# A two-layer transformer on one core: loads of the set-up, the last expert's order, and the engines of the last norm

## The chip, the cores and the metric

The kernel runs on one core of a Trainium2 chip. A core has TensorE (PE in the views; its weight loads are PEld), VectorE (DVE), ScalarE (ACT), GpSimd (POOL) and SyncE (SP, which here only issues DMAs), and 16 DMA engines that move data between the chip's memory (DRAM) and the on-chip buffers. Each engine works through its own queue in order; queues wait for each other on semaphores. The metric is the device time of one execution in microseconds (us); the number given for a kernel is the median of its runs.

## What is computed

Input is x of 4 sequences of 1024 tokens of 256 features. Two blocks follow each other, with a layer norm after each part (cut to its core):

```python
x = norm(x + attention_window_64(x))              # 16 heads of 16, rotary
x = norm(x + sigmoid(xr @ Wr.T) * (square(relu(xk @ Wk.T)) @ Wv.T))   # xr, xk mix x with its predecessor
x = norm(x + linear_attention(x, Wq, Wk, Wv, Wo, random_features))
# last part, a block of its own:
h  = layernorm(x, ln1);  x = x + causal_attention(h @ Wqkv) @ Wproj
h2 = layernorm(x, ln2);  gates = softmax(h2 @ Wgate);  top 2 of 8 experts, capacity 1024 slots each
y_e  = gelu(h2[slots of e] @ W1[e] + b1[e]) @ W2[e] + b2[e]           # e = 0..7, hidden width 1024
x[token] += gate * y_e[slot];   out = norm(x)
```

## The kernel before, in words

The program is four blocks. At the end of a block all engines meet before the next one starts.

1. **Set-up** (`set_up`, L1815 to L1894). SP issues loads of the first sequence's rows (`b_src`), of weights, tables and small vectors, then of the second sequence's rows (`b_y`), then waits and issues ten more weight loads. DVE fills constants, waits, casts four tables to bf16 and finishes three small constants. PE waits, makes the 128x128 product of the random features (`gram`) and turns the rows of the first sequence with 16 transposes (`turn_tiles`, L1467); ACT takes them out of PSUM (L1478). DVE and PE both wait for all loads that stand ahead of `b_y` (L1856, L1873), SP for the same (L1842).
2. **Attention and the first layers** (`attend_and_pass_on`). A planner with a cost for each step writes out the order of every engine. Its first step on PE is the projection of the first sequence (L834); SP's first is the copy of projected queries and keys into the layout for scores (`b_qk<-b_split`, L688). Nothing in this order is changed, apart from what the section on the change tells.
3. **Experts** (`experts`). Per expert e PE makes the hidden layer in 16 groups of 2 matmuls of 512 columns (L1591; `n` is a tile of hidden features, `h` a half of the 1024 slots, `n` outer and `h` inner; the trace has two records for each matmul), into PSUM banks 0 to 3 in turn. ACT applies Gelu to each group (L1624). Then PE turns the next expert's tokens (L1570), waits for all 16 Gelus and makes the 8 tiles of values (128 slots x 256), two to a PSUM bank (L1600). DVE adds the bias and scales by the gate, pair by pair (L1645, L1650). POOL adds each tile to the rows in DRAM with an indirect DMA (L1553), and before each one waits until the one before has landed (`s.summed`, L1551): 64 of them in one chain over the kernel. At the end POOL waits for the last one and the block ends.
4. **Last norm** (`last_norm`). SP reads 4096 rows back in 8 loads of 512 rows (4 tiles of 128 rows; one such load is here called an eighth). For each eighth DVE makes statistics (L1710, L1713), adds epsilon (L1715), ACT makes the inverse root (L1695, L1697), DVE refines it by one Newton step and makes scales and shifts (L1723 to L1727), and the four tiles are scaled, two by DVE (L1730) and two by ACT (L1688). DVE's order is statistics of eighth h, then scale of eighth h-1. SP stores each eighth (L1677) and waits for the stores.

Of the kernel before, what the change touches and what calls it, by code (L numbers as in the profile page):

```python
# [32 lines left out]
P = 128  # L33
# [544 lines left out]
def attend_and_pass_on(nc, u, s, x_dram, later, early_in, slots_gathered, slots_dram, z_dram, x4_dram):  # L578
# [93 lines left out]
    with nc.Block() as block:  # L672
        @block.sync
        def _(sp):
            for x in plan.program["SP"]:
# [50 lines left out]
        def _(pe):  # L726
            for x in plan.program["PE"]:
# [3 lines left out]
                if kind in LAYER_KINDS:  # L731
# [29 lines left out]
                    elif kind == "pj":  # L761
                        done(pe, b, "o_take", x[1] // 2)
                        pe.wait_ge(s.back_read, order[("keep", plan.group_of(b, True, 0), x[1] // 2)] + 1)
                        if b == 0 and x[1] == 0:
                            pe.wait_ge(later, 16 * len(LATER_WEIGHTS))
# [297 lines left out]
        def _(dve):  # L1063
# [11 lines left out]
            for x in plan.program["DVE"]:  # L1075
                kind = x[0]
                if kind in LAYER_KINDS:
# [381 lines left out]
def turn_tiles(pe, src, u, s, chunks=range(NC), half_ready=None):  # L1459


    for h in range(2):
        if half_ready is not None:
            pe.wait_ge(half_ready, h + 1)
        for c in chunks:
# [54 lines left out]
def experts(nc, u, s, slots_gathered, slots_dram, z_dram, w1_dram, b1_dram, w2_dram, b2_dram, x4_dram):  # L1520
# [3 lines left out]
    gathered = (s.x0_gathered, s.x1_gathered)  # L1524
    with nc.Block() as block:
# [13 lines left out]

        @block.gpsimd  # L1540
        def _(pool):
# [3 lines left out]
            gather_tokens(pool, 1, u, s, z_dram)  # L1545
            for e in range(E_):
                for q in range(4):
                    pool.wait_ge(s.y_done, 4 * e + q + 1)
                    for t in range(2):
                        column = CT * e + 2 * q + t  # L1550
                        if column:  # L1551
# [3 lines left out]
                            in_=u.ye[q][:, t, :], in_offset=None, bounds_check=N + P - 1, oob_is_err=True,  # L1555
                            compute_op=ALU.add).then_inc(s.summed, 16)
                    if q == 0 and e + 2 < E_:
                        pool.wait_ge(s.turned, 4 * (e + 1))
                        gather_tokens(pool, e + 2, u, s, z_dram)
            pool.wait_ge(s.summed, 16 * E_ * CT)  # L1560

        @block.tensor
        def _(pe):
# [14 lines left out]
            turn(0)  # L1578
            for e in range(E_):
                pe.wait_ge(weights_in[e % 2], 32 * (e // 2 + 1))  # L1580
                for n in range(NF):
                    for h in range(2):
                        k = 2 * n + h
                        if n == 0:
                            pe.wait_ge(s.taken, 4 * e + 2 * h + 2)
                        if k >= 4:
                            pe.wait_ge(s.h_done, 16 * e + k - 3)
                        elif e:
                            pe.wait_ge(s.y_added, 4 * (e - 1) + k + 1)
                        for c in range(NC):  # L1590
                            ins = pe.matmul(u.psum[:, k % 4, :], u.w1[e % 2][:, c, P * n:P * n + P],  # L1591
                                            u.xgt[:, c, BANK * h:BANK * h + BANK], start=(c == 0), stop=(c == NC - 1))
                        ins.then_inc(s.h_ready, 1)
                if e + 1 < E_:
                    turn(e + 1)
                pe.wait_ge(s.h_done, 16 * (e + 1))
                for q in range(4):
                    for t in range(2):
                        for n in range(NF):
                            ins = pe.matmul(u.psum[:, q, D * t:D * t + D],  # L1600
                                            u.hid[:, n, P * (2 * q + t):P * (2 * q + t + 1)], u.w2[e % 2][:, n, :],
                                            start=(n == 0), stop=(n == NF - 1))
                    ins.then_inc(s.y_ready, 1)

        @block.scalar
        def _(act):
# [10 lines left out]
            for e in range(E_):  # L1617
                if e:
                    act.wait_ge(s.y_ready, 4 * e)
                for n in range(NF):  # L1620
                    for h in range(2):
                        k = 2 * n + h
                        act.wait_ge(s.h_ready, 16 * e + k + 1)
                        act.activation(u.hid[:, n, BANK * h:BANK * h + BANK], u.psum[:, k % 4, :], ACT.Gelu,  # L1624
                                       bias=u.b1[:, NF * e + n:NF * e + n + 1]).then_inc(s.h_done, 1)
                if e + 1 < E_:
                    take(e + 1)

        @block.vector
        def _(dve):  # L1630
# [8 lines left out]
            dve.wait_ge(s.consts_in, 32)  # L1639
            for e in range(E_):  # L1640
                for q in range(4):
                    dve.wait_ge(s.y_ready, 4 * e + q + 1)
                    if e:
                        dve.wait_ge(s.summed, 16 * (CT * (e - 1) + 2 * q + 2))
                    dve.tensor_tensor(u.ye[q][:, :, :], u.psum[:, q, :].rearrange("p (t d) -> p t d", t=2),  # L1645
                                      u.b2b[:, e:e + 1, :].broadcast_to([P, 2, D]), ALU.add).then_inc(s.y_added, 1)
                    dve.wait_ge(s.y_added, 4 * e + q + 1)
                    for t in range(2):
                        column = CT * e + 2 * q + t
# [326 lines left out]
```

## Time and profile before

| | before |
|---|---|
| median of 3 runs | 1938.33 us (1937.84 to 1943.58) |
| profiled execution | 1937.2 us, span from first to last instruction 1935.3 us |
| busy share of the span | PE 89%, DVE 53%, ACT 46%, POOL 43% |
| mean granted TensorE clock | 0.949 of full speed |

How to read it: 1.9 us of the profiled execution lie outside the span. All positions in time below are in us from the span's start. PE is busy 89% of the whole, but there are stretches at either end in which it does nothing. Of the 40 slices of the profile page (48.4 us each) the first has PE at 4 tenths and the last at 0; all three edits of this change lie in those, and in the slice before the last.

### The profile page before, as it was taken

How to read it: one execution, taken by the hardware profiler on the slowest of the kernel's cores; microseconds unless marked ns; L12 is line 12 of the kernel's file. 1: busy time of each engine (PE TensorE's matmuls, PEld its weight loads, DVE VectorE, ACT ScalarE, POOL GpSimd, SP SyncE). 2: the span in 40 equal slices, each digit the busy share in tenths (PEclk: the TensorE clock that was granted, in tenths of full speed). 3: DMA queues.
4: the chain of work that ended last, by engine and by line, in shares of the span. 5: the costliest groups of instructions: out<-in, count | busy, mean ns of one | idle time of the engine just before them, and what ended most of it. 6: DMA issues, size and time to landing. Idle time of an engine off the chain costs nothing. (4 is left out here: it accounts for less than half of the span.)

```text
span 1935.3 us, 32833 instructions
## 1 busy us (share of the span) xinstructions
PE 1727.9 (89%) x10804; PEld 1102.1 (57%) x10804; DVE 1018.1 (53%) x2375; ACT 886.0 (46%) x1855; POOL 827.1 (43%) x1247
## 2 busy tenths in 40 slices
PE   4798998999999899999999999999269999999980
PEld 3565766565467556547755654555237776666750
DVE  2556677858566885847798677785201110001115
ACT  2354464557755364675546466766032222221212
POOL 4573664422377552237664233423533333334210
PEclk9898999999999899999999999999579999999995
DMA  5615235032444213244502214420323323333115
GB/s 186 88 24 66 34 79 67 13 56 67 58 68 92 29 18 50 67 66 68 104 9 34 34 47 66 68 67 2 110 88 81 83 40 72 76 85 84 22 19 179
DMA packets 93058, 124.17 MB, mean 64 GB/s; under 512 B 14064, under 2 KB 63152, under 8 KB 92736
## 3 DMA queue, kind: packets, MB, share of 16 engines
q1 hardware_dynamic: 78560, 105.24, 26.5%
q0 software_dynamic: 14336, 16.83, 5.3%
q8 instruction: 94, 1.54, 0.4%
q14 instruction: 68, 0.56, 0.1%
HBM read 45.70 MB, written 25.56 MB: 37 GB/s over the span
## 5 line engine op out<-in xcount | busy, mean ns | idle before, releaser
L1013 ACT ACTIVATE b_probs<-b_psum 128x512 f32<-128x512 f32 (+3 forms) x896 | 421.2, 538 | 212.0 <-PE b_psum L881 204.6
L1264 DVE TENSOR_REDUCE b_mneg<-b_psum 128x2 f32<-128x384 f32 (+5 forms) x608 | 335.2, 591 | 124.0 <-PE b_psum L868 121.9
L1359 POOL TENSOR_SCALAR_AFFINE_SELECT b_probs<-b_probs 128x512 f32<-128x512 f32 (+1 forms) x400 | 240.1, 612 | 330.3 <-ACT b_probs L1013 320.2
L868 PE MATMUL b_psum<-b_qk 96*128 96x192 bf16 (+4 forms) x1280 | 300.7, 299 | 2.2 <-DVE b_mhalf L1264 1.1
L881 PE MATMUL b_psum<-b_qk 99*128 99x192 bf16 (+5 forms) x1344 | 270.3, 290 | 13.6 <-DVE b_mneg L1264 4.8
L1645 DVE TENSOR_TENSOR b_ye<-b_psum,b_b2b 128x512 f32<-128x512 f32 x32 | 22.1, 692 | 428.2 <-PE b_psum L1600 428.2
L1624 ACT ACTIVATE b_hid<-b_psum,b_b 128x512 f32<-128x512 f32 x128 | 88.0, 687 | 317.3 <-PE b_psum L1591 317.3
L1553 POOL DMA_INDIRECT before_last_norm<-b_ye,b_ids x64 | 99.6, 1557 | 300.0 <-DMA before_last_norm<-b_ye,b_ids 159.9
L1600 PE MATMUL b_psum<-b_w,b_hid 128*128 128x256 f32 x1024 | 222.4, 379 | 0.8 <-ACT b_hid L1624 0.8
L1591 PE MATMUL b_psum<-b_xgt,b_w 128*128 128x512 f32 x512 | 221.2, 592 | 0.0
L1600 PEld LDWEIGHTS b_psum<-b_w,b_hid 128*128 128x128 f32 x1024 | 193.9, 190 | 27.6 <-ACT b_hid L1624 1.6
L897 PE MATMUL b_psum<-b_probs,b_v 128*32 128x192 f32 (+4 forms) x2688 | 198.9, 417 | 0.3 <-POOL b_probs L1359 0.3
L881 PEld LDWEIGHTS b_psum<-b_qk 99*128 99x128 bf16 x1344 | 113.3, 98 | 118.3 <-issue 30.6
L868 PEld LDWEIGHTS b_psum<-b_qk 96*128 96x128 bf16 x1280 | 125.1, 100 | 90.4 <-issue 23.3
L1264 DVE TENSOR_REDUCE b_mhalf<-b_psum 128x1 f32<-128x512 f32 x256 | 165.1, 681 | 17.6 <-PE b_psum L868 17.0
L1375 POOL TENSOR_TENSOR b_rot<-b_product 128x128 f32<-128x128 f32 x256 | 111.5, 468 | 126.1 <-DVE b_product L1247 62.8
L1591 PEld LDWEIGHTS b_psum<-b_xgt,b_w 128*128 128x128 f32 x512 | 97.4, 191 | 119.0 <-issue 118.6
L1247 DVE TENSOR_TENSOR b_product<-b_psum,b_cossin 128x512 f32<-128x512 f32 x128 | 87.9, 687 | 64.6 <-PE b_psum L834 58.4
L834 PE MATMUL b_psum<-b_wqkv,b_xt 128*128 128x384 f32 x320 | 117.8, 494 | 1.4 <-ACT b_xa L924 0.4
L897 PEld LDWEIGHTS b_psum<-b_probs,b_v 128*32 128x32 f32 x2688 | 69.4, 110 | 85.8 <-issue 67.2
L1381 POOL TENSOR_TENSOR b_split<-b_rest,b_split 128x512 bf16<-128x512 f32 x64 | 74.9, 1173 | 42.2 <-ACT b_split L1032 41.5
L861 PE MATMUL b_psum<-b_mask_q,b_id 128*128 128x384 bf16 (+1 forms) x256 | 85.3, 336 | 7.6 <-DMA b_qk<-b_split 6.2
(212 smaller groups left out, 2444.2 us busy)
## 6 DMA issues: line engine op xcount, KB each, us to landing
b_qk<-b_split SPq DMA_DIRECT2D x372, 128.0 KB, 4.9
b_w<-in_W SPq DMA_DIRECT2D x16, 1024.0 KB, 7.8
b_src<-in_x SPq DMA_DIRECT2D x4, 1024.0 KB, 7.6
before_last_norm<-b_early SPq DMA_DIRECT2D x4, 1024.0 KB, 5.1
b_o<-before_last_norm SPq DMA_DIRECT2D x4, 1024.0 KB, 5.4
before_last_norm<-b_o SPq DMA_DIRECT2D x4, 1024.0 KB, 4.5
normed<-b_y SPq DMA_DIRECT2D x4, 1024.0 KB, 4.5
b_rows<-before_last_norm SPq DMA_DIRECT2D x8, 512.0 KB, 7.7
```

The costliest lines, as they stand in the source:

```text
L834: ins = pe.matmul(u.psum[:, plan.bank[x], 0:384].rearrange("p (a g y) -> p a g y", a=3, g=2), x_rows[:, c, P * t:P * t + P], (u.wqkv0 if n ...
L868: ins = pe.matmul(out[:, i, :], q[0:KS, h, P * t:P * t + P], q[0:KS, HG + h, a:e], start=not last, stop=True, skip_group_check=True)
L881: ins = pe.matmul(out[:, i, :], q[0:KM, HG + h, P * t:P * t + P], q[0:KM, h, a:e], start=True, stop=True, skip_group_check=True)
L897: ins = pe.matmul(u.ot[32 * h:32 * h + 32, a:e], u.v[:, g % 4, t, (HD + 1) * h:(HD + 1) * h + 32], probs_of(cell, a, e)[:, h, :], start=(t ...
L1013: act.activation(probs_of((g, h2, t), a, e)[:, heads[0]:heads[-1] + 1, :], bank, ACT.Exp, scale=SCALE).then_inc(s.exp_done, 1)
L1264: dve.tensor_reduce(out, in_bank(("max",) + x[1:], heads, e - a), AX.X, ALU.max, negate=True).then_inc(s.max_read, 1)
L1359: ins = pool.affine_select(out=block, in_=block, pattern=[[0, HG], [1 if ahead else -1, z - y]], compare_op=ALU.is_ge, fill=none, base=y - ...
L1375: ins = pool.tensor_tensor(out[:, :, :, HALF * y:HALF * y + HALF], straight[:, :, :, HALF * y:HALF * y + HALF], crossed[:, :, :, HALF * (1 ...
L1553: pool.indirect_dma_start(out=x4_dram, out_offset=bass.IndirectOffsetOnAxis(ap=u.ids[:, column:column + 1], axis=0), in_=u.ye[q][:, t, :], ...
L1591: ins = pe.matmul(u.psum[:, k % 4, :], u.w1[e % 2][:, c, P * n:P * n + P], u.xgt[:, c, BANK * h:BANK * h + BANK], start=(c == 0), stop=(c ...
L1600: ins = pe.matmul(u.psum[:, q, D * t:D * t + D], u.hid[:, n, P * (2 * q + t):P * (2 * q + t + 1)], u.w2[e % 2][:, n, :], start=(n == 0), s ...
L1624: act.activation(u.hid[:, n, BANK * h:BANK * h + BANK], u.psum[:, k % 4, :], ACT.Gelu, bias=u.b1[:, NF * e + n:NF * e + n + 1]).then_inc(s ...
```

## The change

**Set-up.** The identity (`b_id`) and the first sequence's rows in two halves are issued first and have semaphores of their own; PE turns the rows as each half lands, before it makes `gram`. What DVE and `gram` wait for is five loads: `wqkv0`, `cossin`, `blocks`, the tables and the random features, the last now one DMA that repeats its source in place of eight. Then come `b_y` and the 16 small loads that nothing in the set-up needs, counted on the semaphore `later`. The ten weight loads move into the next block's SP queue, ahead of its first step. DVE's two additions of 1 (`bk`, `bq_plus`) move to the first `y1` step of the first sequence, behind a wait for everything on `later`; PE's wait ahead of the first `pj` covers the same count.

**Last expert.** For e = 7 the hidden groups run with `h` outer: ten groups (all eight of the first half of slots, two of the second), then the values of tiles 0 to 3, then the six other groups, then tiles 4 to 7. The values go to banks 4 to 7 and 0, tiles 6 and 7 are emptied singly. The other seven experts are as before.

**Last norm.** It stands in the experts' block: SP waits for the last landing itself and reads on. The Newton step, the scales and the shifts move from DVE to POOL, as six small operations (the combined one becomes two). Of the four tiles ACT scales two, POOL one, DVE one. DVE's order is statistics of h, then one tile of h-1. The load of ACT's function table stands behind the last Gelu.

```diff
 def turn_tiles(...):
     for h in range(2):
+        pe.wait_ge(rows_in[h], 16 if h else 32)
...
 # set_up, SP
-            sp.dma_start(u.src[:, :, :], ...).then_inc(loaded, 16)
-            for n in names: ...                      # 14 loads
-            ... tables, bk, bv, bo, 8 x rft, slots, 2 x spare_rows, all on loaded
-            ... u.y on early_in
-            sp.wait_ge(loaded, 16 * (count + 3))
-            for n in LATER_WEIGHTS: ...
+            sp.dma_start(u.id32[:, :], a["id32"]).then_inc(rows_in[0], 16)
+            for h in range(2):
+                sp.dma_start(u.src[:, 4 * h:4 * h + 4, :], x_rows[:, 4 * h:4 * h + 4, :]).then_inc(rows_in[h], 16)
+            for n in first:                          # wqkv0 cossin blocks
+                sp.dma_start(made[n][:], a[n]).then_inc(loaded, 16)
+            sp.dma_start(tables, a["tables"]).then_inc(loaded, 16)
+            sp.dma_start(u.rft[:, :].rearrange("p (j d) -> p j d", d=HD), a["rft"].unsqueeze(1).broadcast_to([64, P // HD, HD])
+                         ).then_inc(loaded, 16)
+            ... u.y on early_in; LATER_SMALL, LATER_ROWS, slots, 2 x spare_rows on later
 # set_up, PE
-            pe.wait_ge(loaded, 16 * (count + 3))
-            gram; turn_tiles(pe, u.src, u, s)
+            turn_tiles(pe, u.src, u, s, rows_in)
+            pe.wait_ge(loaded, 16 * count)
+            gram
 # attend_and_pass_on, SP
+            for n in LATER_WEIGHTS:
+                sp.dma_start(made[n][:], arrays[n]).then_inc(later, 16)
             for x in plan.program["SP"]:
 # attend_and_pass_on, DVE, kind y1
+                        if not b and not x[1]:
+                            dve.wait_ge(later, LATER_COUNT)
+                            dve.tensor_scalar(u.bk[:, :], u.bk[:, :], 1.0, None, ALU.add)
+                            chained(dve.tensor_scalar(u.bq_plus[:, :], u.bq[:, :], 1.0, None, ALU.add))
...
 # experts, PE, last expert
+                parts = list(enumerate(hidden_order(e)))
+                for k, (n, h) in parts[:NF + 2]:
+                    hidden(e, k, n, h)
+                pe.wait_ge(s.h_done, 16 * e + NF)
+                for tiles in pieces_of(e)[:2]:
+                    values(e, tiles)
+                for k, (n, h) in parts[NF + 2:]:
+                    hidden(e, k, n, h)
                 pe.wait_ge(s.h_done, 16 * (e + 1))
+                for tiles in pieces_of(e)[2:]:
+                    values(e, tiles)
...
 # experts, SP: the last norm's reads
+            sp.wait_ge(s.summed, 16 * E_ * CT)
+            for h in range(HALVES):
+                sp.dma_start(u.rows[:, 4 * h:4 * h + 4, :], rows(x4_dram, h)).then_inc(rows_in[h], 16)
 # experts, POOL, behind the last scatter
-            pool.wait_ge(s.summed, 16 * E_ * CT)
+            link = dve_chain(pool, last.chain)
+            for h in range(HALVES):
+                pool.wait_ge(last.root_ready, h + 1)
+                link(pool.tensor_tensor(scales, root, root, ALU.mult))
+                ... three more of the Newton step, each behind link
+                link(pool.tensor_tensor(u.shifts[:, four], u.last_mv[:, four, 0], scales, ALU.mult))
+                pool.tensor_scalar(u.shifts[:, four], u.shifts[:, four], -1.0, None, ALU.mult).then_inc(last.scale_ready, 1)
+                i = 4 * h + 2
+                pool.tensor_scalar(u.rows[:, i, :], u.rows[:, i, :], u.last_mv[:, i, 0:1], u.scales[:, i:i + 1],
+                                   ALU.subtract, ALU.mult).then_inc(last.pool_ready, 1)
```

On SP, at the head of the program, this stood before (L1828 to L1844 is the set-up; a name ahead of `<-` is what is written):

```order
L1830 DMA b_src<-in_x 128x8x256
L1832 DMA b_wqkv<-in_wqkv 128x1536
...
L1837 DMA b_rft<-in_rft 64x16 x8
L1838 DMA slots<-in_empty 16x1024
L1840 DMA normed<-in_spare_rows 16x2048
L1840 DMA before_last_norm<-in_spare_rows 16x2048
L1841 DMA b_y<-in_x 128x8x256
L1844 DMA b_wout<-in_wout 128x512
...
L1844 DMA b_wqkv<-in_wqkv 128x1536
L1827 UNCONDITIONAL_BRANCH
```

and this stands there now:

```order
L1866 DMA b_id<-in_id 128x128
L1868 DMA b_src<-in_x 128x4x256 x2
L1870 DMA b_wqkv<-in_wqkv 128x1536
L1870 DMA b_cossin<-in_cossin 128x1024
L1870 DMA b_blocks<-in_blocks 128x128
L1871 DMA b_o<-in_tables 128x768
L1872 DMA b_rft<-in_rft 64x8x16
L1874 DMA b_y<-in_x 128x8x256
...
L1863 UNCONDITIONAL_BRANCH
L679 UNCONDITIONAL_BRANCH
L682 DMA b_wout<-in_wout 128x512
```

The end of the block (the branch) has moved ahead of the ten weight loads; ahead of it stand 25 DMAs now, 41 before.

On PE, the end of the program before (the last expert: 16 groups of hidden, then all values):

```order
L1591 MATMUL b_psum<-b_xgt,b_w 128x512 x32
L1600 MATMUL b_psum<-b_w,b_hid 128x256 x64
L1525 UNCONDITIONAL_BRANCH
```

and now:

```order
L1651 MATMUL b_psum<-b_xgt,b_w 128x512 x20
L1659 MATMUL b_psum<-b_w,b_hid 128x256 x32
L1651 MATMUL b_psum<-b_xgt,b_w 128x512 x12
L1659 MATMUL b_psum<-b_w,b_hid 128x256 x32
```

The same 96 matmuls, with half of the values moved ahead of 12 of the hidden ones.

On POOL, behind the last scatters, where before only the block's end stood, there is now for each eighth:

```order
L1603 DMA before_last_norm<-b_ye,b_ids 4224x256 x22
L1615 TENSOR_TENSOR b_scales<-b_last_root 128x4
L1616 TENSOR_TENSOR b_scales<-b_scales,b_last_var 128x4
L1617 TENSOR_SCALAR b_scales<-b_scales 128x4
L1618 TENSOR_TENSOR b_scales<-b_scales,b_last_root 128x4
L1619 TENSOR_TENSOR b_shifts<-b_last_mv,b_scales 128x4
L1620 TENSOR_SCALAR b_shifts<-b_shifts 128x4
L1622 TENSOR_SCALAR b_rows<-b_rows,b_last_mv,b_scales 128x256
```

Seven operations of an eighth that stood on DVE (five small ones and two tiles) are now seven on POOL and one on DVE.

## Rows read from the trace of the kernel before

**Rows 1.** Waits, 0 to 30 us: total us, times, longest.

```profile
PE b_psum L1874 <- DMA before_last_norm<-in_spare_rows: 19.7, 1, 19.7
```

**Rows 2.** Timeline, 0 to 40 us: start, duration, engine, what, [idle before].

```profile
0.80 0.44 SPq L1830 DMA_DIRECT2D b_src<-in_x  x1
...
10.56 5.05 SPq L1837 DMA_DIRECT2D b_rft<-in_rft  x8
...
20.59 0.28 DVE L1863 TENSOR_TENSOR b_bg<-b_psum,b_blocks 128x128 f32<-128x128 f32 x1
...
24.02 0.45 SPq L1844 DMA_DIRECT2D b_wqkv<-in_wqkv  x1
...
24.99 7.13 PE L834 MATMUL b_psum<-b_wqkv,b_xa 128*128 128x384 f32 x16 [0.94 <-PEq L1827]
...
32.40 2.75 PE L834 MATMUL b_psum<-b_wqkv,b_xa 128*128 128x384 f32 x8
...
36.24 3.85 SPq L688 DMA_DIRECT2D b_qk<-b_split  x6
```

**Rows 3.** Windows: stretch, us, busy per engine, granted clock, DMA share, GB/s.

```profile
0.00:5.00 5.00, 0.00 (x0) 0.00 (x0) 2.63 (x8) 1.28 (x1) 4.40 (x6) 1.00 0.54 172
5.00:10.00 5.00, 0.00 (x0) 0.00 (x0) 0.00 (x0) 0.00 (x0) 5.00 (x2) 1.00 1.05 337
```

**Rows 4.** Timeline of the last expert, 1820 to 1900 us.

```profile
1822.31 27.63 PE L1591 MATMUL b_psum<-b_xgt,b_w 128*128 128x512 f32 x64
...
1850.72 27.89 PE L1600 MATMUL b_psum<-b_w,b_hid 128*128 128x256 f32 x128 [0.78 <-ACT b_hid L1624]
1857.93 0.69 DVE L1645 TENSOR_TENSOR b_ye<-b_psum,b_b2b 128x512 f32<-128x512 f32 x1 [33.89 <-PE b_psum L1600]
...
1860.04 1.54 POOL L1553 DMA_INDIRECT before_last_norm<-b_ye,b_ids  x1 [22.02 <-DVE b_ye L1650]
...
1871.74 0.69 DVE L1645 TENSOR_TENSOR b_ye<-b_psum,b_b2b 128x512 f32<-128x512 f32 x1 [5.55 <-PE b_psum L1600]
...
1878.23 1.59 POOL L1553 DMA_INDIRECT before_last_norm<-b_ye,b_ids  x1 [3.05 <-DMA before_last_norm<-b_ye,b_ids]
...
1891.60 1.54 POOL L1553 DMA_INDIRECT before_last_norm<-b_ye,b_ids  x1 [2.85 <-DMA before_last_norm<-b_ye,b_ids]
1899.65 7.48 SPq L1673 DMA_DIRECT2D b_rows<-before_last_norm  x8
```

**Rows 5.** Timeline of the last norm, 1900 to 1936 us.

```profile
1903.88 1.40 DVE L1710 BATCH_NORM_STATS2 b_last_bn<-b_rows 128x6 f32<-128x256 f32 x4 [23.89 <-DMA b_rows<-before_last_norm]
...
1905.73 0.17 DVE L1715 TENSOR_SCALAR b_last_var<-b_last_mv 128x4 f32<-128x4 f32 x1
...
1906.17 0.20 ACT L1697 ACTIVATE b_last_root<-b_last_ln 128x4 f32<-128x4 f32 x1
...
1909.25 1.40 DVE L1710 BATCH_NORM_STATS2 b_last_bn<-b_rows 128x6 f32<-128x256 f32 x4
...
1912.68 1.40 DVE L1710 BATCH_NORM_STATS2 b_last_bn<-b_rows 128x6 f32<-128x256 f32 x4
...
1930.85 1.09 ACT L1688 ACTIVATE b_rows<-b_rows,b_shifts,b_scales 128x256 f32<-128x256 f32 x2 [0.42 <-DVE b_shifts L1727]
```

**Rows 6.** Timeline, POOL, 582 to 585 us: its small operations, each behind a semaphore.

```profile
582.57 0.25 POOL L1309 CAST b_mparts<-b_mneg 128x16 bf16<-128x16 f32 x1
...
583.55 0.27 POOL L1312 TENSOR_TENSOR b_mparts<-b_mrest,b_mparts 128x16 bf16<-128x16 f32 x1
```

**Rows 7.** One line, L1348 and L1309: count, duration ns min/median/max.

```profile
L1348 POOL TENSOR_SCALAR b_xa<-b_xa x16: 1476/1487/1509, 233.5 to 1100.8; 128x512 f32<-128x512 f32 x16
...
L1309 POOL CAST b_mparts<-b_mneg x64: 248/254/712, 51.6 to 1313.8; 128x16 bf16<-128x16 f32 x64
```

**Rows 8.** Timeline, POOL and DVE, 573 to 578 us: two operations side by side.

```profile
576.40 1.27 POOL L1330 TENSOR_TENSOR b_o<-b_y,b_o 128x512 f32<-128x512 f32 x1
...
576.52 1.18 DVE L1103 TENSOR_SCALAR b_kvm_mt<-b_kvm_mt 128x4 f32<-128x4 f32 x1
```

More of the change, by code:

```diff
@@ L1545, in _ @@
             gather_tokens(pool, 1, u, s, z_dram)
+            piece = 0
             for e in range(E_):
[L1547 to L1550, printed above, removed]
+                for tiles in pieces_of(e):
+                    piece += 1
+                    pool.wait_ge(s.y_done, piece)
+                    for t in tiles:
+                        column = CT * e + t
                         if column:
@@ L1578, in _, with hidden @@
             turn(0)
+            def hidden(e, k, n, h):
+                if n == 0:
+                    pe.wait_ge(s.taken, 4 * e + 2 * h + 2)
+                if k >= 4:
+                    pe.wait_ge(s.h_done, 16 * e + k - 3)
+                elif e:
+                    pe.wait_ge(s.y_added, 4 * (e - 1) + k + 1)
+                for c in range(NC):
+                    ins = pe.matmul(u.psum[:, k % 4, :], u.w1[e % 2][:, c, P * n:P * n + P],
+                                    u.xgt[:, c, BANK * h:BANK * h + BANK], start=(c == 0), stop=(c == NC - 1))
+                ins.then_inc(s.h_ready, 1)
@@ L1579, in _, with values @@
+            def values(e, tiles):
+                for t in tiles:
+                    for n in range(NF):
+                        ins = pe.matmul(u.psum[:, bank_of(e, t), D * (t % 2):D * (t % 2) + D], u.hid[:, n, P * t:P * (t + 1)],
+                                        u.w2[e % 2][:, n, :], start=(n == 0), stop=(n == NF - 1))
+                ins.then_inc(s.y_ready, 1)
             for e in range(E_):
                 pe.wait_ge(weights_in[e % 2], 32 * (e // 2 + 1))
[L1581 to L1593, printed above, removed]
@@ L1605, in _ @@
+                for tiles in pieces_of(e)[2:]:
+                    values(e, tiles)
         @block.scalar
@@ L1708, in statistics @@
+            link = dve_chain(dve, last.dve_chain)
+            def apply(h):
+                dve.wait_ge(last.scale_ready, h + 1)
+                i = 4 * h + 3
+                dve.tensor_scalar(u.rows[:, i, :], u.rows[:, i, :], u.last_mv[:, i, 0:1], u.scales[:, i:i + 1],
+                                  ALU.subtract, ALU.mult).then_inc(last.dve_ready, 1)
+            for h in range(HALVES):
                 dve.wait_ge(rows_in[h], 16)
@@ L1821, in set_up @@
     gram = ctx.enter_context(nc.semaphore("gram_ready"))
-    names = "wqkv0 cossin id32 blocks iota next_token mur muk bq ln1g ln1b ln2g ln2b wgate".split()
-    count = len(names) + 5 + P // HD
+    rows_in = [ctx.enter_context(nc.semaphore(f"first_rows{h}_in")) for h in range(2)]
+    first = "wqkv0 cossin blocks".split()
+    count = len(first) + 2
     bf16_tables = (u.id16[:, :], u.mask_q[:, :, :], u.causal_q[:, :], u.upto[:, :])
@@ L1926, in two_layers @@
             u = named(made)
[L1927 to L1929 removed]
+            experts(nc, u, moe, last, slots_gathered, slots_dram, z_dram, a["W1"], a["b1"], a["W2"], a["b2"], x4_dram, out)
 def kernel(**inputs):
```

195 lines of the change are left out of this document (85 added, 110 removed).

## The prediction

> **What bounds the kernel now.** I read the waits at the start first: PE, which is 89% busy over the whole, stands for 19.7 us until the last of the set-up's loads has landed [rows 1]. Then the timeline of the first 40 us, for what SP does meanwhile: between 0.80 and 10.56 it issues 19 DMAs, one every 0.514 us, and the eight tiny ones of the random features cost it 5.05 us, 0.63 each [rows 2]. The DMA engines are near full from 5 to 10 us (share 1.05, 337 GB/s; 172 GB/s in the first 5) [rows 3], so the bulk is in by about 10 us and what PE waits for afterwards is SP's own pace. The block ends for another reason: SP's tenth weight load goes out at 24.02 and ends at 24.47, and PE's first projection starts at 24.99 [rows 2]. That is the first thing to move.
>
> At the other end I read the timeline of the last expert [rows 4]. PE finishes at 1878.6, but POOL's scatters are a chain, each waiting for the landing of the one before: eight from 1860.04 to 1891.60, one every 4.51 us. They start late because all 16 hidden groups (27.6 us) stand ahead of the first values. From the last issue (1891.60 + 1.54) the landing takes as long as those before it, 2.9 us, so it is in at 1896.05. SP's first read of the norm goes out only at 1899.65: 3.6 us for the end of the block. From there to the end of the span are 35.65 us, and the norm's timeline shows DVE with an eighth every 3.43 us (statistics start 1909.25, 1912.68) [rows 5], without a gap. So the tail is scatter chain, block end, DVE.
>
> **Set-up: −10.2 us.** Ahead of the block's end stand 25 DMAs: 20 of the kind that took 0.514 us, and five (random features, b_y, three with 16 partitions) that I price at 0.63 like the features [rows 2]: 10.3 + 3.2 + 0.8 = 14.3. From SP's last issue to PE's start were 0.5 us (24.47 to 24.99); so PE starts at 14.8, against 24.99. Is anything later than SP? The five loads with rows and identity ahead of them are 2.9 MB; rows 3 give 2.5 MB in the first 10 us, so they are in near 11.5 with the landing, and DVE's casts and `b_bg` behind them took from the release at 19.7 to 20.87, 1.2 us: 12.7. PE's 16 transposes lie ahead of that. SP keeps the block. The ten weight loads, 4.9 us of SP, now run from about 14.8 to 19.7; the first thing behind them, the copies to b_qk at 36.24, comes at 26 at the earliest, so they cost nothing there, and their 3.1 MB take 9.2 us at 337 GB/s, over by 25. DVE's two moved additions (under 0.5 us together) and its new wait come over 100 us later, when all this has long landed. Bounds: without any queueing it is 10.6. If DMAs of many pieces hold SP up as the eight reads of the norm did (7.48 us for eight, 0.93 each instead of 0.51 [rows 4]), b_y and the next few cost 2 us more. PE's first 16 matmuls took 7.13 us where the later eight took 2.75, so 1.6 us over that pace; a longer or shorter slow phase moves that by as much. So −7 to −10.8.
>
> **Middle: 0.** No order is changed. All of it is shifted; I allow 1 us each way.
>
> **Last expert: −4.4 us.** Ten groups of 1.73 us (27.63/16) end at 1839.6; a pair of value tiles takes 7.0 (27.89/4): the first is ready at 1846.6, and 2.1 us later (DVE 1857.93 to scatter 1860.04) the first scatter, 1848.8, instead of 1860.04. Tiles 0 to 3 are through at 1866.8. Then the chain must wait: the third pair needs all of the hidden work and three pairs of values, the same PE work as before, so DVE starts on it at 1871.74 as before and the scatter at 1873.85; before it was 1878.23. This is what is late next, not the chain. The three behind it, at 4.46 each, and the landing give 1891.7 against 1896.05. Emptying tiles 6 and 7 singly gains nothing: 7 is ready at about 1880.7 and its turn is at 1887. Gain bounded by 4.0 and 4.8.
>
> **Block end: −3.5 us.** SP waits for the same landing and issues the read itself; 0.1 us for the semaphore in place of 3.6. If part of the 3.6 is landing and not block end, the gain is less: 2.5 to 3.6. The read goes out at 1891.8.
>
> **Last norm: +1.0 us.** First the parts that stay: read to first statistics 4.23, statistics of the first eighth 2.02, root 0.5, and at the end ACT's two tiles 1.1 and 3.4 from the end of ACT (1931.94) to the end of the span [rows 5]. Between them the period of an eighth counts seven times. DVE needs 1.93 for statistics (2.02 less the overlap with the next) and 0.36 for a tile: 2.3, where it needed 3.43. But POOL now has six small operations and a tile. Its small ones come every 0.33 us in a chain of the same form (582.57 to 583.55 in three steps) [rows 6]: 1.98. Its tile is a tensor_scalar of 256 columns; one of 512 takes 1.487 [rows 7]; with 0.2 fixed that is 0.85. Sum 2.83, so POOL sets the pace. On top comes that the two engines block each other. A 128x4 tensor_scalar on DVE, which takes 0.17 by itself [rows 5], took 1.18 and ended with the POOL operation that had begun 0.12 before it (576.40 + 1.27) [rows 8], and POOL's smallest operations, 0.254 in the median, reach 0.712 [rows 7]. In the new order DVE's tile of h-1 and POOL's tile of h-1 are released by the same semaphore: one waits for the other, and DVE's 0.36 then falls on POOL's next small operation; in some eighths DVE's 128x4 operation, on which the root hangs, falls under POOL's tile. I add 0.36 for the first and 0.16 for the second: 3.35. Phase: 4.23 + 2.02 + 0.5 + 7 × 3.35 + 1.98 + 1.1 + 3.4 = 36.7, against 35.65. DMA doesn't bound it: 8.4 MB at 337 GB/s are 25 us. Bounds by the nearest rows: DVE's pace of 2.3 gives 29.3 (−6.3); POOL's small operations at 0.35, its tile as long as the one of 512 and 0.52 of blocking give a period of 4.1 and 42.1 (+6.5). I take the middle since both of its terms scale from a row of the same kind.
>
> [...] The Trainium skill, "GPSIMD Engine Reference", "Engine selection", calls one-input operations on GpSimd roughly line-rate, and its "Elementwise" section gives 1.03 cycles an element at 1.2 GHz; that would be 0.44 us for 512 columns, and rows 7 show 1.487. By the page POOL's tile would be about 0.4 us, an estimate, and the phase some 3 us shorter; this is one way into rival (a).
>
> **Sum.** −10.2 − 4.4 − 3.5 + 1.0 = −17.1 against the profiled execution's 1937.2: 1920 us. That execution lies 1.1 below the median of the runs, within what runs of one kernel differ.
>
> **Rivals.** (a) POOL keeps up: its tile or the blocking is cheaper and the period comes near 2.5. For it: DVE's own tile is only 0.36, and some operations beside each other didn't collide. Against it: rows 6 to 8. Phase 30.8, total 1914. (b) POOL's tile with two operations and scalars per partition costs what one of 512 columns does, 1.49: period 4.0 to 4.1, total 1925.5. For it: no row shows such a tile on POOL. (c) The set-up doesn't do what it says: SP is held by full queues and the first matmuls stay slow for longer, so that 5 us of 10 remain: 1925. For it the eight reads of 0.93 each [rows 4]; against it that before 19 loads went out at an even pace while the engines were full. (d) Slower than before: every small POOL operation of the norm runs at the longest seen, 0.712 + 0.08, so 4.75 for six, with 1.49 and 0.52 a period of 6.8 us: the phase is 4.23 + 2.02 + 0.5 + 47.6 + 4.75 + 4.5 = 63.6, 28 more than before, against 18.1 gained: 1947. It decides from a period of about 5.8 on. Only operations beside others were that long, and the median is 0.254.
>
> **How the numbers follow.** A measurement of this kernel can tell about 0.3%, 6 us, from no change. My forecast (1917 to 1923) has 0.52, (a) 0.2, (b) 0.13, (c) 0.10, (d) 0.02; 0.03 is left for a time between 1932 and 1944 from several terms at their bounds. The range that holds 8 in 10 runs from (a) to beyond (b) and (c): 1912 to 1928. Faster by over 0.3%: 0.95; the same 0.03; slower 0.02.
>
> **What would show it.** In the profile after: PE's first projection at 14.8 (10 to 12 would say SP doesn't hold the block, 17 or more (c)); SP's weight loads over before the first b_qk copy; two groups of four scatters in the last expert with a gap ahead of the fifth, which starts near 1863.6 (1873.85 less the 10.2 of the set-up); SP's read within 0.2 us of the last landing; in the norm, POOL without gaps, an eighth every 3.35 us, DVE's tensor_scalars of 0.17 and 0.4 us stretched by up to a POOL tile. The sum is wrong if DVE and not POOL runs without gaps in the norm, if the last eighth leaves less than 30 or more than 40 us after the read, or if the block's 3.6 us turn up between the last landing and the read.

## The result and the profile after

| | before | after |
|---|---|---|
| median of the runs | 1938.03 us (5 runs, 1936.08 to 1943.58) | 1923.58 us (5 runs, 1918.47 to 1926.44) |
| profiled execution | 1937.2 us, span 1935.3 | 1918.47 us, span 1916.7 |
| mean granted clock in it | 0.949 | 0.953 |

The ratio of the times is 0.9917, 95% interval 0.9898 to 0.9936: faster by 14.5 us in the median, where the forecast of 1920 us meant 18. Six further runs of the same kernel on another occasion gave a median of 1921.48 us (1914.64 to 1928.27), ratio 0.9922 [0.9898, 0.9946]. The profiled execution was the fastest of its five; its span is 18.6 us shorter, and I trace these 18.6 us place by place.

Set-up, timeline of the kernel after, 0 to 40 us (start, duration, engine, what, idle before). It answers to [rows 2]:

```profile
5.17 0.82 SPq L1874 DMA_DIRECT2D b_y<-in_x  x1
...
5.41 3.67 PE L1478 MATMUL b_psum<-b_id,b_src 128*128 128x128 f32 x16 [5.41 <-DMA b_src<-in_x]
6.03 3.91 SPq L1876 DMA_DIRECT2D b_iota<-in_iota  x1
...
9.98 0.45 SPq L1876 DMA_DIRECT2D b_next_token<-in_next_token  x1
...
12.35 0.23 DVE L1896 CAST b_id<-b_o 128x128 bf16<-128x128 f32 x1 [8.30 <-DMA b_rft<-in_rft]
...
13.20 0.29 DVE L1898 TENSOR_TENSOR b_bg<-b_psum,b_blocks 128x128 f32<-128x128 f32 x1
...
17.12 0.59 SPq L1881 DMA_DIRECT2D before_last_norm<-in_spare_rows  x1
18.36 0.33 SPq L682 DMA_DIRECT2D b_wout<-in_wout  x1
...
18.40 6.80 PE L842 MATMUL b_psum<-b_wqkv,b_xa 128*128 128x384 f32 x16 [5.24 <-PEq L1863]
...
22.66 0.64 SPq L682 DMA_DIRECT2D b_wqkv<-in_wqkv  x1
...
29.32 10.85 SPq L696 DMA_DIRECT2D b_qk<-b_split  x17
```

PE starts at 18.40, not at 24.99: 6.6 us gained. DVE was done at 13.5 and PE's transposes at 9; SP keeps the block until 17.7. One DMA cost it the difference: the small load of `b_iota`, issued right behind `b_y`, held SP for 3.91 us, where the ones behind it take about 0.45.

Last expert, timeline 1810 to 1920 us, which answers to [rows 4]:

```profile
1815.02 17.33 PE L1651 MATMUL b_psum<-b_xgt,b_w 128*128 128x512 f32 x40
...
1841.41 1.54 POOL L1603 DMA_INDIRECT before_last_norm<-b_ye,b_ids  x1 [10.65 <-DVE b_ye L1750]
...
1855.01 1.55 POOL L1603 DMA_INDIRECT before_last_norm<-b_ye,b_ids  x1 [2.96 <-DMA before_last_norm<-b_ye,b_ids]
...
1857.24 14.08 PE L1659 MATMUL b_psum<-b_w,b_hid 128*128 128x256 f32 x64 [0.78 <-ACT b_hid L1702]
1864.46 0.69 DVE L1746 TENSOR_TENSOR b_ye<-b_psum,b_b2b 128x512 f32<-128x512 f32 x1 [16.88 <-PE b_psum L1659]
...
1866.57 1.54 POOL L1603 DMA_INDIRECT before_last_norm<-b_ye,b_ids  x1 [10.01 <-DVE b_ye L1750]
...
1880.00 1.55 POOL L1603 DMA_INDIRECT before_last_norm<-b_ye,b_ids  x1 [2.84 <-DMA before_last_norm<-b_ye,b_ids]
...
1883.58 7.05 SPq L1580 DMA_DIRECT2D b_rows<-before_last_norm  x8
```

PE enters the last expert 7.3 us earlier than before (1815.02 against 1822.31), the last scatter goes out 11.6 earlier: 4.3 come from the order. The fifth scatter waits 10.01 us for DVE, as forecast. From the last scatter to SP's read are 3.58 us, before 8.05: 4.5 from the end of the block.

Last norm, one eighth in the timeline of 1900 to 1912 us, which answers to [rows 5]:

```profile
1901.35 0.20 POOL L1615 TENSOR_TENSOR b_scales<-b_last_root 128x4 f32<-128x4 f32 x1
...
1901.63 0.20 POOL L1616 TENSOR_TENSOR b_scales<-b_scales,b_last_var 128x4 f32<-128x4 f32 x1
...
1902.61 0.17 DVE L1771 TENSOR_SCALAR b_last_var<-b_last_mv 128x4 f32<-128x4 f32 x1
1902.76 0.23 POOL L1620 TENSOR_SCALAR b_shifts<-b_shifts 128x4 f32<-128x4 f32 x1
...
1902.97 1.23 POOL L1622 TENSOR_SCALAR b_rows<-b_rows,b_last_mv,b_scales 128x256 f32<-128x256 f32 x1
1903.03 0.64 DVE L1760 TENSOR_SCALAR b_rows<-b_rows,b_last_mv,b_scales 128x256 f32<-128x256 f32 x1 [0.25 <-POOL b_shifts L1620]
...
1904.17 0.20 POOL L1615 TENSOR_TENSOR b_scales<-b_last_root 128x4 f32<-128x4 f32 x1
```

POOL has no gap: six small operations from 1901.35 to the tile at 1902.97 (1.62), then the tile, next eighth at 1904.17. The period is 2.82 us and POOL's, before it was 3.43 and DVE's. From the read to the end of the span are 33.1 us against 35.65: 2.5 gained. The sum of the four is 6.6 + 4.3 + 4.5 + 2.5 = 17.9. The missing 0.7 is the middle (all between PE's first projection and its first matmul of the last expert), where the lead of 6.6 us has become 7.3. That small number hides larger ones, to which the second half of the experiments goes.

### The profile page after: what moved, and what is told of

It reads as the page before. It is cut to its first block and busy times, and to the rows that moved or that the text cites. A ratio compares the mean times of both kernels' runs of the same rounds, so it can differ in the third digit from the quotient of the medians.

```text
span 1916.7 us, 32827 instructions
## 1 busy us (share of the span) xinstructions
PE 1728.4 (90%) x10804; PEld 1100.5 (57%) x10804; DVE 1012.8 (53%) x2328; ACT 884.5 (46%) x1855; POOL 845.8 (44%) x1303
## 5 line engine op out<-in xcount | busy, mean ns | idle before, releaser
L1746 DVE TENSOR_TENSOR b_ye<-b_psum,b_b2b 128x512 f32<-128x512 f32 (+1 forms) x33 | 22.3, 676 | 427.8 <-PE b_psum L1659 427.8
```

## Experiments: the parts alone

All were timed beside the kernel before, 4 to 9 runs each; its median there was 1937.64 us for e1 to e4, 1937.03 for after_again and e5 to e7, and 1937.27 for e8 to e11.

**e1_setup.** The new set-up with the experts and the norm of before.

> The set-up part of the change alone; experts and last norm as before. Theory (SP held up by full DMA queues while it issues the small loads): PE's first projection at 18.4 us as in the whole change, one small load issue of some 4 us, everything behind shifted by 6.6 to 7.3 us: about 1930.5 us against 1937.5 of before. Rival (the whole change's gain in the first 20 us is partly lost again in the score stage, where PE waits for copies and the granted clock changes): shift of 6.6 us at 20 us but under 5 us at 1300 us, total above 1932.5.

**e2_order.** Only the order of the last expert and the way its tiles are emptied:

```diff
+    return ... if e + 1 < E_ else [(n, h) for h in range(2) for n in range(NF)]
+                for k, (n, h) in parts[:NF + 2]: hidden(e, k, n, h)
+                for tiles in pieces_of(e)[:2]: values(e, tiles)
```

> Only the last expert's order and its emptying; set-up and last norm (a block of its own) as before. Theory: the chain of scatters has a gap ahead of the fifth and ends 4.4 us earlier: about 1933 us. Rival (the chain alone sets the end, and earlier values only lengthen waits): the last scatter starts where it did, 1891.6 us, no gain.

**e3_norm.** Only the norm in the experts' block on three engines; set-up and order of before.

> Only the last norm of the change: in the experts' block and over three engines; set-up and the last expert's order as before. Theory: the first read goes out 2.0 us after the last scatter's issue ends instead of 6.5 us (4.5 us gained) and the norm lasts 33.1 us from the read instead of 35.65 (2.5 us gained): about 1930.5 us. Rival (POOL's indirect DMAs just before slow its first operations): the norm takes over 34 us.

**e4_join.** Only the joined block, the norm divided between DVE and ACT as before:

```diff
-    with nc.Block() as block:      # last_norm's own
+            sp.wait_ge(s.summed, 16 * E_ * CT)
```

> The last norm stands in the experts' block, but with before's division of work (DVE refines the root and scales two tiles, ACT two); set-up and order as before. Theory: only the 4.5 us of the block's end go, the norm keeps DVE's 3.43 us an eighth and 35.6 us from read to end: about 1933 us. Rival (the block's end only hid a landing that SP must wait for anyway): under 2.5 us gained, 1935 or more.

| | median us (range) | ratio [95%] | last scatter to read | read to end of span |
|---|---|---|---|---|
| before | 1937.64 (1935.39 to 1940.84) | | 8.05 | 35.65 |
| e1_setup | 1928.18 (1926.52 to 1938.02) | 0.9957 [0.9944, 0.9971] | 7.8 | 35.7 |
| e2_order | 1932.00 (1931.42 to 1933.12) | 0.9972 [0.9962, 0.9983] | 7.9 | 35.8 |
| e3_norm | 1930.72 (1928.64 to 1931.56) | 0.9963 [0.995, 0.9976] | 3.7 | 33.3 |
| e4_join | 1932.37 (1928.66 to 1934.55) | 0.9971 [0.996, 0.9982] | 3.8 | 35.3 |

The last scatter and the read of e4_join in its timeline:

```profile
1891.82 1.54 POOL L1592 DMA_INDIRECT before_last_norm<-b_ye,b_ids  x1 [2.98 <-DMA before_last_norm<-b_ye,b_ids]
1895.63 1.47 SPq L1569 DMA_DIRECT2D b_rows<-before_last_norm  x3
```

So each part pays by itself. Joining the blocks is worth 4.2 us and leaves the norm nearly as it was (35.3 against 35.65); what the three engines add in e3_norm is 2.0 us of phase (33.3 against 35.3); the order in e2_order, corrected for PE's entry that was 1.3 us earlier (1820.99), is 5.5 − 1.3 = 4.2. Only e1_setup is uneven: its nine runs reach from 1926.5 to 1938.0, and its profiled one, at 1937.59, shows PE 6.9 us ahead at the first projections and 0.5 us behind at the last expert. Everything the set-up gained was lost on the way in that execution. It meets the rival of its expectation (no lead left at 1300 us, total above 1932.5), while the median meets the theory. The other three came within 1 us of the totals expected, and their rivals are out by the rows.

At the two ends the parts add up: 6.9 + 4.2 + 4.3 + 2.4 = 17.8 us in the four profiles, against 17.9 for the whole change. The medians don't: 9.5 + 5.6 + 6.9 = 22.0 us for e1 to e3, against 14.5 and 15.6 for the two sets of runs of the whole. The difference lies in the middle; why it fell out against the whole change is not shown.

## Experiments: the disputed terms

**e5_y_last.** What held SP for 3.9 us? The changed kernel, with one load moved:

```diff
             ... rft
-            sp.dma_start(u.y[:, :, :], ...).then_inc(early_in, 16)
             ... LATER_SMALL, LATER_ROWS, slots, 2 x spare_rows
+            sp.dma_start(u.y[:, :, :], ...).then_inc(early_in, 16)
```

> Changed kernel with the load of the second sequence's rows (b_y) moved behind all other loads of the set-up; the count of loads ahead of the block's end stays 25. Theory A (SP was held 3.9 us at the small load behind b_y, because b_y's pieces fill the queues): the hold goes or moves to the block's last issue, PE's first projection starts at 14.5 to 15.5 instead of 18.40, and if the middle keeps it the median falls by 3 to 4 us to about 1920. Rival B (the queues are full of everything issued so far, not of b_y): SP is held at some other load by about as much, PE starts at 17.5 to 18.5, no change.

Its timeline, 0 to 16 us:

```profile
4.71 0.76 SPq L1872 DMA_DIRECT2D b_rft<-in_rft  x1
...
5.51 1.15 SPq L1875 DMA_DIRECT2D b_iota<-in_iota  x1
...
14.57 0.58 SPq L1881 DMA_DIRECT2D b_y<-in_x  x1
15.56 0.33 SPq L682 DMA_DIRECT2D b_wout<-in_wout  x1
...
15.60 6.80 PE L842 MATMUL b_psum<-b_wqkv,b_xa 128*128 128x384 f32 x16 [2.42 <-PEq L1863]
```

Theory A holds. The same small load behind `b_rft` costs 1.15, none costs more than that in the block, and PE starts at 15.60: 2.8 us earlier with the same 25 DMAs. In the five other traces with `b_y` in its old place the load behind it took 3.6 to 4.3 us. Median 1916.47 us (1912.31 to 1924.37), ratio 0.9891 [0.9868, 0.9915]; it is 5.0 us below the changed kernel's 1921.48 in the same rounds, of which these 2.8 are shown. Which resource was full isn't shown; that it was `b_y`, issued while the bulk ahead of it was in flight, is: in e11_best_more below `b_y` is issued at 13.43, behind all of that, and the load after it takes 0.57.

**e6_act3.** The norm's third tile from POOL to ACT:

```diff
-                pool.tensor_scalar(u.rows[:, i, :], ...).then_inc(last.pool_ready, 1)
-                for i in range(4 * h, 4 * h + 2):
+                for i in range(4 * h, 4 * h + 3):      # ACT
```

> Changed kernel with the norm's third tile given to ACT (ACT three, DVE one, POOL only the six small operations). Theory (POOL paces the norm at 2.82 us an eighth, 1.60 of small operations and 1.22 of tile): the pace falls to DVE's, statistics 1.97 and a tile of 0.36 plus its wait, 2.3 to 2.5, or ACT's (0.45 for the root, 1.6 for three tiles); over seven eighths 2.3 to 3.6 us, read to end 29.5 to 31 us instead of 33.1. Rival (the loads or stores bound the phase, 8.4 MB in about 25 us): under 1 us gained.

One eighth in its timeline:

```profile
1899.17 1.40 DVE L1763 BATCH_NORM_STATS2 b_last_bn<-b_rows 128x6 f32<-128x256 f32 x4
1899.25 1.57 ACT L1708 ACTIVATE b_rows<-b_rows,b_shifts,b_scales 128x256 f32<-128x256 f32 x3
...
1901.10 0.41 DVE L1757 TENSOR_SCALAR b_rows<-b_rows,b_last_mv,b_scales 128x256 f32<-128x256 f32 x1
...
1901.42 1.40 DVE L1763 BATCH_NORM_STATS2 b_last_bn<-b_rows 128x6 f32<-128x256 f32 x4
```

The pace is now DVE's, 2.25 to 2.32, and the phase 29.2 us (read 1885.89, end 1915.1) instead of 33.1. Neither loads nor stores bound the phase at 33.1; here DVE once waits 0.20 us for a load. Median 1916.69 us (1913.96 to 1917.23), ratio 0.9888 [0.9867, 0.991].

**e7_singles.** Tiles 4 and 5 singly, 5 in a bank that the hidden groups have left:

```diff
-    ... [(0, 1), (2, 3), (4, 5), (6,), (7,)]
+    ... [(0, 1), (2, 3), (4,), (5,), (6,), (7,)]
-    return ... else 4 + t // 2 if t + 1 < CT else 0
+    return ... else (4, 4, 5, 5, 6, 1, 7, 0)[t]
```

> Changed kernel with tiles 4 and 5 of the last expert emptied singly too, each in a PSUM bank of its own. Theory (the fifth scatter waited 10.0 us for the pair of tiles 4 and 5): DVE gets tile 4 after 3.5 us of values instead of 7.0, its own work on a single tile is shorter by 0.3 to 0.6, the fifth scatter goes out 3.5 to 4.1 us earlier (5.9 to 6.5 us gap instead of 10.0), all behind it likewise: the median falls by 3.5 to 4. Rival (the chain is the limit in both halves and the gap only idle time that comes back later): the read goes out where it did.

Timeline 1825 to 1925 us:

```profile
1852.36 14.08 PE L1659 MATMUL b_psum<-b_w,b_hid 128*128 128x256 f32 x64 [0.78 <-ACT b_hid L1702]
1856.12 0.42 DVE L1746 TENSOR_TENSOR b_ye<-b_psum,b_b2b 128x256 f32<-128x256 f32 x1 [13.39 <-PE b_psum L1659]
...
1857.69 1.54 POOL L1603 DMA_INDIRECT before_last_norm<-b_ye,b_ids  x1 [6.05 <-DVE b_ye L1750]
...
1862.77 1.55 POOL L1603 DMA_INDIRECT before_last_norm<-b_ye,b_ids  x1 [3.53 <-DMA before_last_norm<-b_ye,b_ids]
```

Counted from PE's last values, the fifth scatter goes out after 5.3 us instead of 9.3 (1857.24 to 1866.57), the gap is 6.05 instead of 10.01; the sixth comes 5.1 behind it instead of 4.6, so the read gains 3.1 (23.2 us after PE's last values begin, instead of 26.3). Median 1912.46 us (1910.48 to 1917.37), ratio 0.9879 [0.9856, 0.9902]. That is 9.0 us below the changed kernel's 1921.48, three times what the edit gains: the rest is the middle, of which the next part tells.

## Experiments: the middle

**after_again.** The changed kernel once more.

> The changed kernel unaltered, to see what its middle does in further executions. If the middle is fixed by the program (a longer dependency somewhere), PE's n-th matmul stands at every point where it stood in the first profile, within 1 us: 7.5 us ahead of before at 140 us, 3.5 to 5 ahead between 160 and 560, 7.3 ahead from 1138 us on. If it is the half-clock stretches that fall differently in each execution, the shift at the two ends is the same (6.6 at 25 us) but steps of 2 to 5 us stand at other places, and the times spread over 4 to 8 us as they did (1918.5 to 1926.4).

It stood 5.9 us ahead of before at 140 us, 1.8 at 560 and 8.9 at the last expert; in the first profile 7.6, 3.4 and 7.3. The steps stand at the same places, their sizes differ by up to 3 us; neither expectation holds in full. What a step is can be seen on the same four matmuls, with the wait ahead of them. In the kernel before, then in the changed one, its repetition and e7_singles:

```profile
155.78 1.96 PE L655 MATMUL b_psum<-b_early,b_wk 128*128 128x512 f32 x4 [1.33 <-DVE b_early L1142]
```

```profile
148.16 3.75 PE L661 MATMUL b_psum<-b_early,b_wk 128*128 128x512 f32 x4 [1.68 <-DVE b_early L1154]
```

```profile
149.90 3.75 PE L661 MATMUL b_psum<-b_early,b_wk 128*128 128x512 f32 x4 [1.61 <-DVE b_early L1154]
```

```profile
150.33 3.36 PE L661 MATMUL b_psum<-b_early,b_wk 128*128 128x512 f32 x4 [1.68 <-DVE b_early L1154]
```

1.96 us is full clock, 3.75 half (granted 0.5, the lower of the two levels, 1.2 GHz). The work is the same and PE had waited before it in each. It goes the other way further on; windows of before and then of after (stretch, us, busy of PE, PEld, DVE, ACT, POOL, granted clock, DMA share, GB/s):

```profile
620.00:660.00 40.00, 35.57 (x290) 26.64 (x286) 28.66 (x102) 12.44 (x27) 17.73 (x28) 0.83 0.40 61
660.00:700.00 40.00, 35.05 (x150) 22.29 (x150) 34.56 (x72) 19.14 (x42) 24.05 (x32) 0.91 0.01 1
```

```profile
620.00:660.00 40.00, 33.63 (x266) 23.47 (x258) 31.36 (x105) 10.64 (x25) 18.04 (x25) 0.91 0.39 52
660.00:700.00 40.00, 38.20 (x189) 24.62 (x190) 35.63 (x75) 24.84 (x54) 24.50 (x36) 1.00 0.01 2
```

**e8_delay.** The kernel before, started later:

```diff
-            sp.dma_start(u.src[:, :, :], ...)
+            for j in range(NT): sp.dma_start(u.src[:, j:j + 1, :], ...)
-            sp.dma_start(u.y[:, :, :], ...)
+            for j in range(NT): sp.dma_start(u.y[:, j:j + 1, :], ...)
```

> The kernel before with nothing changed but its start: the loads of b_src and b_y are issued in eight pieces of 128 rows each, 14 more DMAs at 0.45 to 0.65 us, so PE's first projection moves from 25.0 to 31.5 to 34. Theory P (the middle depends on where its work falls in time: stretches of half clock come and go with the start alone): the shift of PE's matmuls does not stay what it is at 30 us; it changes by 1.5 us or more somewhere between 140 and 700 us, as in every trace with the new set-up, and the runs spread wider than the kernel before's. Rival A (the changes of the middle come from what the new set-up moved there, DVE's two additions and the ten weight loads): the shift of 7 to 9 us stays within 1.5 us to the end, and the median is 7 to 9 us above before.

The four matmuls in it:

```profile
163.39 3.42 PE L655 MATMUL b_psum<-b_early,b_wk 128*128 128x512 f32 x4 [2.16 <-DVE b_early L1142]
```

PE started at 30.63, earlier than I had expected. The delay was 5.6 us there, 7.6 at 140 us and 9.1 at 258; from then on it stayed within 0.4. The same four matmuls are slow in it, though no work of the middle was touched, so rival A is out as the whole of it. But the delay isn't needed for such a step either. In e4_join, where everything ahead of the last expert is as before and PE starts only 0.35 us later, the four are slow as well:

```profile
154.02 3.47 PE L655 MATMUL b_psum<-b_early,b_wk 128*128 128x512 f32 x4 [2.14 <-DVE b_early L1142]
```

Both lose 2.2 us between 152 and 159 us of before, while e2_order and e3_norm, unchanged there too, show 1.96 and lose nothing. So the step comes without any edit to the middle; that the start decides it isn't shown. The other half of theory P is wrong: the six runs lie within 1943.35 to 1945.98, no wider than before's. Median 1943.72, ratio 1.0034 [1.0022, 1.0047]. The profiled execution is 2.2 us above that; the median's delay of 6.45 us is only 0.8 more than PE's at the start.

**e9_adds.** The changed kernel with the two additions taken out of the middle and put back into the set-up:

```diff
-                            dve.wait_ge(later, LATER_COUNT)
-                            dve.tensor_scalar(u.bk[:, :], ...); chained(dve.tensor_scalar(u.bq_plus[:, :], ...))
+            dve.tensor_scalar(u.bk[:, :], ...)           # set_up, after the casts
+            dve.tensor_scalar(u.bq_plus[:, :], ...).then_inc(fixed, 1)
```

> Changed kernel with DVE's two additions back in the set-up, and the loads of bq and bk ahead of the wait there; no wait on the later loads in DVE's first y1. Rival A (the additions cost the middle): the loss of 1.5 to 3.4 us between matmuls 894 and 911 (152 to 158 us of before) that all six traces of the new set-up show is gone, the median is 2 to 3 us lower than the changed kernel's. Theory P: the loss at that place stays in 1.5 to 3.4 us, the median within 2 us of the changed kernel's 1921 to 1924.

The lead falls from 4.9 to 1.9 us between 150 and 160 us of before: the step is there without the additions. Median 1923.18 us (1919.66 to 1928.70), ratio 0.9928 [0.9911, 0.9944], the changed kernel's own. The additions cost nothing that shows.

From the granted-clock records of each trace I added up the time at half clock between PE's first projection and the last expert, and set it beside what the middle did (the delay against before at the last expert, less that at the first projection; a minus is time gained):

| kernel | half clock, against before's 143 us | middle |
|---|---|---|
| e2, e3, e4 | −3, +3, 0 | −1.4, −0.6, −0.7 |
| after, after_again | −3, −9 | −0.7, −2.3 |
| e1_setup, e5_y_last | +15, +14 | +7.4, +5.9 |
| e6_act3, e7_singles | +5, −20 | +1.3, −6.2 |
| e8_delay, e9_adds | +7, +3 | +3.1, +4.3 |
| e10_best, e11_best_more | −6, −10 | −3.2, −2.7 |

A straight line through the 13 traces gives 0.38 us for each us at half clock, correlation 0.94. With the four matmuls this makes the half clock the likely cause of most of the middle; no run set the clock by itself. All nine traces with the new set-up, wherever `b_y` and the additions stand, lose 1.4 to 3.1 us between 150 and 160 us of before, and six of them get back 2.0 to 3.4 us between 660 and 680. Where they don't, 3.5 of 9.4 us of the start's gain are left (e5_y_last), 1.5 of 5.8 (e9_adds) or none (e1_setup).

## A better version

**e10_best** joins e5, e6 and e7. **e11_best_more** also moves four loads into the next block's queue:

```diff
# set_up
-            ... slots, 2 x spare_rows, u.y
# attend_and_pass_on, SP
+            sp.dma_start(u.y[:, :, :], ...).then_inc(early_in, 16)
             for n in LATER_WEIGHTS: ...
+            ... slots, 2 x spare_rows
```

> The three improvements together on the changed kernel: b_y's load last in the set-up, ACT with three tiles of the norm and DVE with one, tiles 4 and 5 emptied singly. If they add, the start gains 2.8, the last expert 3.3 and the norm 3.8 us: 9.9 us, against the changed kernel's 1921 to 1924 this is 1911 to 1914, with the spread of the middle (about 4 us each way) around it.

> As the kernel before this one in the call, with the loads of slots, the two of spare rows and b_y moved out of the set-up into the next block's queue of SP (b_y ahead of the weight loads, the others behind them). SP ends its block at 13.3 instead of 15.15, PE's first projection starts at 13.7 to 14.0 instead of 15.6 (DVE's last operation of the block ends at 13.5, so no earlier). If the middle keeps it the median is 1.6 to 1.9 us lower, 1909 to 1912; if the weight loads now push back the copies to b_qk (26.5), the gain is gone by 27 us.

The start of e11_best_more, timeline 0 to 45 us:

```profile
12.85 0.29 DVE L1895 TENSOR_TENSOR b_bg<-b_psum,b_blocks 128x128 f32<-128x128 f32 x1
13.43 0.38 SPq L681 DMA_DIRECT2D b_y<-in_x  x1
...
13.47 7.53 PE L846 MATMUL b_psum<-b_wqkv,b_xa 128*128 128x384 f32 x16 [0.65 <-PEq L1864]
13.86 0.57 SPq L683 DMA_DIRECT2D b_wout<-in_wout  x1
...
20.59 0.59 SPq L686 DMA_DIRECT2D before_last_norm<-in_spare_rows  x1
...
25.11 19.95 SPq L700 DMA_DIRECT2D b_qk<-b_split  x30
```

e10_best: 1905.52 us (1904.30 to 1915.52), ratio 0.9853 [0.9831, 0.9874]. e11_best_more: 1904.01 us (1903.11 to 1907.81), ratio 0.9832 [0.9817, 0.9846]. Both were below their forecasts of 1911 to 1914 and 1909 to 1912, which had added the gains at the two ends and put the middle at nothing. In the profiled execution of e10_best the start gained 3.4 us on the changed kernel's first profile (14.99 against 18.40), PE's last values to the read 3.4, the norm 4.1 (29.0), together 10.9 of a span shorter by 13.5; the rest is the middle. In e11_best_more PE starts at 13.47, right behind DVE's last operation of the set-up, and the copies to `b_qk` are not pushed back; its median is 1.5 us lower than e10's, with overlapping intervals.

## Why the prediction came out as it did

The time was forecast at 1920 and came at 1923.58, within the range of 1912 to 1928 and just above the narrow one of 1917 to 1923. But three of its five terms were off, in both directions, two of them beyond their own bounds (set-up and block end).

- **Set-up, −10.2: measured −6.6.** The step that failed is the issue pace, "five ... that I price at 0.63". The small load behind `b_y` took 3.91, and PE's start at 18.40 is past the 17 that was named as the sign of rival (c). I had named the mechanism, in the bounds (2 us for `b_y` and the next few) and as rival (c), and took the even pace of 19 loads before as evidence against it; but there `b_y` stood last, and nothing of the block queued behind it. e5_y_last shows that its place is the cause. The other steps held: the five loads in at 12.35 (forecast about 11.5, DVE through at 12.7, measured 13.5), weight loads over before the first copy.
- **Middle, 0 (±1): −0.7 in the first profile, −6 to +7 over the traces.** The sign changes from trace to trace; the size of the allowance was wrong. "No order is changed. All of it is shifted" assumed that the same work runs at the same clock. e8_delay and e4_join contradict it (the four matmuls at 3.42 and 3.47 us in place of 1.96). The other four runs of the changed kernel have spans of 1918.5 to 1924.7 us at a mean clock of 0.950 to 0.946, and the median lies 5 us above the profiled execution.
- **Last expert, −4.4: measured −4.3** (4.2 alone), with the gap ahead of the fifth scatter where it was forecast. That emptying 6 and 7 singly gains nothing fits too (DVE is through with tile 7 at 1872.3, ahead of the scatter of tile 6 at 1875.62); the pair to split was the one I had called what is late next (e7_singles, 3.1 us).
- **Block end, −3.5: measured −4.5** (4.2 to 4.3 alone). I took the landing after the last issue for 2.9 us and left all of it in place; from the last issue's end to the read are now 2.03 us, so the landing was over sooner than the chain's usual spacing says.
- **Last norm, +1.0: measured −2.5.** POOL sets the pace, as forecast, but at 2.82 and not 3.35. Two terms failed. The small operations were priced at 0.33 from [rows 6] and come every 0.28 (0.20 each): −0.38 an eighth with the sixth. And DVE's 128x4 operation was never caught under POOL's tile, it is 0.17 in all eight: −0.16. What I had put for the tile and its collision with DVE's, 0.85 + 0.36 = 1.21, is what the tile takes, 1.22; whether as a collision isn't known. The sum without both allowances for blocking, 2.83, is the period that was measured, but its parts are not: the small operations are 0.38 too high in it, the tile 0.37 too low. Seven times 0.54 is 3.8 us, against 3.6 by which the phase came out shorter (33.1 for 36.7). This lies between the forecast and rival (a), whose price for POOL was not reached.

By the Trainium skill, "SBUF — State Buffer", section "SBUF: two separate sides", the port pair that DVE and GpSimd (POOL) share is locked: whichever starts first, a GpSimd operation or a DVE operation in a two-port mode, keeps it for its whole instruction and the other fully blocks. No run shows in which mode DVE's tile ran. Here DVE's tile began 0.06 us behind POOL's and ended 0.53 before it, at 0.65 instead of 0.41 in e6_act3: either the order of the two was not that of the records, or it wasn't such a lock. POOL's tile never ran without DVE's beside it, so how much of its 1.23 us is its own stays open; it wasn't tried.

Rival (b) (period 4.0) and (d) are out by the same rows. That the total came near is in part luck, for the errors nearly cancelled: 3.6 us less from the set-up, 3.5 more from the norm, 1.0 more from the block end; with the middle's 0.7 the profiled execution's span became 18.6 us shorter, forecast 17.1. The median, 5 us above it, is where the middle's spread comes in.

## What to carry to other kernels

Put a load of many rows that nobody needs soon behind the small ones, and look in the profile for a single issue that is long: here the DMA that stood there wasn't the one to blame, the one ahead of it was. When an engine takes over work, count its own chain before giving it a tile as well: here six small operations were enough for POOL, and the tile was cheaper on ACT. A gain at the head of a long kernel is not safe until the end: look at the granted clock of several executions before believing a difference of 5 us.

## What was not expected of the hardware

- The time at half clock in one program of 1.9 ms ranged from 123 to 158 us over 14 traces in which PE's work between set-up and last expert was the same, and with it the middle moved by −6 to +7 us. What decides where the clock falls is open: it differs between kernels that are the same up to the last expert (before, e4_join), and the two additions are not the cause (e9_adds). Whether the ten weight loads have a part was not tried, nor is it shown why six of the nine sets of runs with the new set-up spread over 8 to 14 us, the other three over 3 to 7 and e8_delay over 2.6.
- The end of a block behind a chain of indirect DMAs cost 4.2 to 4.5 us on SP's path (8.05 us from the last scatter's issue to the read, against 3.6 to 3.8 when joined).
- POOL's 128x256 tensor_scalar with two operations took 1.23 us beside DVE's; ACT does such a tile in 0.52 (three in 1.57).
